# Three graph layers with the weight product behind the aggregation, without transposes, in two halves of the source tiles

## The reference, cut to what matters

```
h = relu(layernorm(x))
for i in range(3):
    hw   = h @ Ws[i]
    agg  = einsum('bij,bie->bje', adj, hw)      # A' (h W)
    h    = relu(layernorm(agg + bs[i] + h) * gammas[i] + betas[i])
x = x + h
# then: additive attention, 4-head attention, normalised graph convolution,
# each on relu(layernorm(x)) and with adj as mask or matrix
```

## Time and profile before

| what | value |
|---|---|
| median of 3 runs | 13956.94 us (13955.01 to 13957.97) |
| profiled execution, span | 13956.8 us |
| TensorE busy | 12838.3 us (92%) |
| VectorE busy | 9919.4 us (71%) |
| ScalarE busy | 9332.8 us (67%) |
| GpSimd busy | 313.1 us (2%) |
| chain that ended last: TensorE, issue, VectorE | 70%, 17%, 8% |
| adjacency products of the graph layers (L1015), busy | 1359.7 us, 3072 records |

### The profile page before, as it was taken

One profiled execution on the slowest core, in us unless ns is written; L12 is line 12 of the kernel. 1 busy time (PEld: TensorE's weight loads), 2 busy tenths in 40 slices (PEclk: granted clock), 3 DMA queues, 4 the chain that ended last, 5 costly groups with the idle time before them and its releaser, 6 DMA issues.

```text
span 13956.8 us, 273781 instructions
## 1 busy us (share of the span) xinstructions
PE 12838.3 (92%) x111489; PEld 6395.6 (46%) x111489; DVE 9919.4 (71%) x13831; ACT 9332.8 (67%) x9144; POOL 313.1 (2%) x377
## 2 busy tenths in 40 slices
PE   7998989989899898998989989899898998989989
PEld 3333843338433384333833338333383333833338
DVE  3887738877388763887638876388764887648876
ACT  2886628866288663886638866388663886638866
POOL 0000000000000000000000000000000000000000
PEclk9999989999899999999989999899999999989999
DMA  1001300013000130001300013000130001300012
GB/s 61 19 16 43 115 34 19 16 43 118 31 19 19 41 118 30 19 19 43 122 24 18 19 43 127 21 17 19 43 127 22 16 19 45 128 18 16 19 46 85
DMA packets 124596, 636.11 MB, mean 46 GB/s; under 512 B 15504, under 2 KB 49936, under 8 KB 49936
## 3 DMA queue, kind: packets, MB, share of 16 engines
q1 hardware_dynamic: 92944, 420.58, 8.6%
q0 software_dynamic: 18432, 134.23, 2.5%
q10 hardware_dynamic: 12288, 67.13, 2.3%
HBM read 546.38 MB, written 8.39 MB: 40 GB/s over the span
## 4 chain that ended last, share of the span: by engine, by line
PE 70%; issue 17%; DVE 8%; ACTq 2%; POOL 1%; ACT 1%; DMA 0%; DVEq 0%; SPq 0%; POOLq 0%
PE ps L913 44%; PE ps L955 7%; PE ps L968 4%; PE ps L926 4%; PE ps L1094 3%; PE ps L946 3%; DVE E L619 3%; ACTq L499 2%; DVE E L618 2%; PE ps L862 2%; DVE E L620 2%; PE ps L1082 1%; POOL rstd L311 1%; PE ps L977 1%; PE ps L1042 0%
## 5 line engine op out<-in xcount | busy, mean ns | idle before, releaser
L913 PE MATMUL ps<-E,a_win 128*32 128x512 f32 x65536 | 7182.0, 594 | 157.5 <-DVE E L620 88.9
L913 PEld LDWEIGHTS ps<-E,a_win 128*32 128x32 f32 x65536 | 2131.0, 110 | 5025.1 <-issue 4771.4
L404 ACT ACTIVATE E<-Q,ka 128x2048 f32<-128x2048 f32 x2048 | 4076.8, 1991 | 0.0
L403 ACT ACTIVATE E<-Q,ka 128x1024 f32<-128x1024 f32 x2048 | 2347.6, 1146 | 668.5 <-PE ps L913 666.4
L618 DVE TENSOR_SCALAR E<-Q,kd 128x2048 f32<-128x2048 f32 x2048 | 2627.6, 1283 | 186.6 <-PE ps L913 151.6
L619 DVE TENSOR_SCALAR E<-Q,kd 128x2048 f32<-128x2048 f32 x2048 | 2623.3, 1281 | 0.0
L620 DVE TENSOR_SCALAR E<-Q,kd 128x1024 f32<-128x1024 f32 x2048 | 1531.7, 748 | 0.0
L334 ACT ACTIVATE PT<-ps 128x512 f32<-128x512 f32 x1792 | 1001.9, 596 | 752.0 <-PE ps L862 478.7
L1015 PE MATMUL ps<-adj_res,HW 128*128 128x512 f32 x3072 | 1359.7, 602 | 24.0 <-ACT HW L334 16.3
L687 DVE CUSTOM_DVE_ANT_0 T<-ps,adj_ring 128x2048 f32<-128x2048 f32 x512 | 1173.3, 2292 | 251.6 <-PE ps L946 210.8
L432 ACT ACTIVATE T<-T,nmin 128x2048 f32<-128x2048 f32 x512 | 1021.9, 1996 | 304.6 <-issue 304.6
(11 more groups left out here) (111 smaller groups left out, 8100.4 us busy)
## 6 DMA issues: line engine op xcount, KB each, us to landing
adj_ring<-in_adj SPq DMA_DIRECT2D x384, 1024.0 KB, 4.8
adj_res<-in_adj POOLq DMA_DIRECT2D x128, 1024.0 KB, 6.7
qst<-qh ACTq DMA_DIRECT2D x64, 256.0 KB, 5.0
qst<-ql ACTq DMA_DIRECT2D x64, 256.0 KB, 5.0
kst<-kh ACTq DMA_DIRECT2D x64, 256.0 KB, 5.0
kst<-kl ACTq DMA_DIRECT2D x64, 256.0 KB, 5.0
X<-in_x SPq DMA_DIRECT2D x128, 64.0 KB, 1.9
out_x<-HW SPq DMA_DIRECT2D x8, 1024.0 KB, 9.7
```

Of the source, the lines that this page charges most:

```text
L403: nc.scalar.activation(E[:, s + 2, N // 2:N], Q2[:, N // 2:N], ACT.Relu, bias=ka[:, u, 32 + m:33 + m])
L404: nc.scalar.activation(E[:, s + 3, :], Q2[:, :], ACT.Relu, bias=ka[:, u, 48 + m:49 + m]).then_inc(e_act, 1)
L913: last = mm(ps[QROWS * grp:QROWS * (grp + 1), 4 * u + c, :], win, E[:, s + grp, c * CH:(c + 1) * CH], start=(m == 0), stop=(m == QUADS - 1 ...
```

## The change

The graph layers compute (A'h)W. H itself, with rows on partitions as it comes out of the relu, is the stationary operand of the adjacency products. The aggregate has features on partitions, which is what the product with W wants of its stationary operand, and that product comes out with rows on partitions. So both sets of transposes go, and so does HW as an operand; the buffer HW now holds relu(Z) + bias (`biased`), which is added to the product. The adjacency products of a layer run over all four chunks of columns with source tiles 0 to 7 first, and then over all four with tiles 8 to 15. Layer norm in the graph layers goes by chunks of four tiles. The first normalise of X goes to HT (where Z lies), so that the relu writes H from HT; the relu of the last layer moves into VectorE's residual pass. The bias table `b0` is [128, 3, 128] in place of [128, 3], and the semaphore for A is split into one for each half of its tiles.

```diff
@@ -24,16 +24,27 @@
 MASK_ADD = 1e22
 MASK_DOT = 1e9
 SCALE = float(1.0 / (HD ** 0.5))
-LNS = LAYERS + 4
-HTS = LAYERS + 2
-HEV = LAYERS + 3
+HTS = 2
+HEV = LAYERS + 2
 HALF = 8
 
 
-LN_ORDER = [(i, half) for i in range(LAYERS) for half in range(2)]
-LN_ORDER += [(LAYERS, 0), (LAYERS + 1, 0), (LAYERS, 1), (LAYERS + 1, 1)]
-LN_ORDER += [(i, half) for i in range(LAYERS + 2, LNS) for half in range(2)]
-DVE_STEPS = 2 * LNS + 4 * LAYERS + 7
+def half_of(half):
+    return range(half * HALF, (half + 1) * HALF)
+
+
+def chunk_of(c):
+    return range(c * TPC, (c + 1) * TPC)
+
+
+LN_X, LN_1, LN_2, LN_3 = 0, LAYERS + 1, LAYERS + 2, LAYERS + 3
+LN_STEPS = [(LN_X, half_of(half)) for half in range(2)]
+LN_STEPS += [(l, chunk_of(c)) for l in range(1, LAYERS) for c in range(NC)]
+LN_STEPS += [(i, chunk_of(c)) for c in range(NC) for i in (LAYERS, LN_1)]
+LN_STEPS += [(i, half_of(half)) for i in (LN_2, LN_3) for half in range(2)]
+LN_COUNT = len(LN_STEPS)
+LN_EARLY = LN_COUNT - 4
+DVE_STEPS = 68
 STEPS = NT * HEADS
 
 
...
@@ -360,16 +368,9 @@
                 evac_ht(b, i, 3)
                 after(3)
 
-            def evac_hw(b, l, g):
-                if l == 0 and g == 0:
-                    act.wait_ge(out_done, b * 16 + 16)
-                act.wait_ge(hw_ps, b * (LAYERS * NC) + l * NC + g + 1)
-                evac(HW[:, g * CH:(g + 1) * CH], ps[:, 4 + g, :]).then_inc(hw_sb, 1)
-
             def evac_agg(b, l, c):
                 act.wait_ge(agg_ps, b * (LAYERS * NC) + l * NC + c + 1)
-                nc.scalar.activation(AGG[:, c * CH:(c + 1) * CH], ps[:, c, :], ACT.Identity,
-                                     bias=b0[:, l:l + 1]).then_inc(agg_sb, 1)
+                evac(AGG[:, c * CH:(c + 1) * CH], ps[:, c, :]).then_inc(agg_sb, 1)
 
             def evac_q1(b, c):
                 act.wait_ge(qk1_ps, b * 6 + c + 1)
@@ -461,19 +462,21 @@
             act.sem_inc(hb_sb, NT)
             with act.Fori(0, NB) as b:
                 Hf = H[:, :, :].rearrange("p t d -> p (t d)")
-                h_section(b, 0, 0, Hf, lambda g: evac_hw(b, 0, g))
+                for g in range(NC):
+                    relu(b, 0, HT, g)
                 for l in range(LAYERS):
-                    for c in range(NC - 1):
+
+                    evac_agg(b, l, 0)
+                    evac_agg(b, l, 1)
+                    for c in range(2, NC):
+                        if l < LAYERS - 1:
+                            relu(b, l + 1, HT, c - 2)
                         evac_agg(b, l, c)
                     if l < LAYERS - 1:
-                        h_section(b, l + 1, l + 1, HT, lambda g: evac_hw(b, l + 1, g), lambda: evac_agg(b, l, NC - 1))
-                    else:
-                        for g in range(NC):
-                            if g == 2:
-                                evac_agg(b, l, NC - 1)
-                            relu(b, LAYERS, HT, g)
-
-                h_section(b, LAYERS, LAYERS + 1, Hf, lambda c: evac_q1(b, c))
+                        relu(b, l + 1, HT, 2)
+                        relu(b, l + 1, HT, 3)
+
+                h_section(b, 0, LAYERS, Hf, lambda c: evac_q1(b, c))
                 for c in range(2):
                     act.wait_ge(qk1_ps, b * 6 + 4 + c + 1)
                     evac(K2[:, c * CH:(c + 1) * CH], ps[:, c, :]).then_inc(qk1_sb, 1)
...
@@ -553,49 +556,67 @@
             nc.vector.tensor_copy(w1t2[:, DG:P], ps[:, 0, 0:DG])
             nc.vector.tensor_copy(w2t[:, :], ps[:, 0, DG:P]).then_inc(const_rdy, 1)
 
-            def tiles_of(half):
-                return range(half * HALF, (half + 1) * HALF)
-
-            def norm_stats(b, half, src):
-
-                for t in tiles_of(half):
+            def ln_at(i, over):
+                return LN_STEPS.index((i, over)) + 1
+
+            def norm_stats(b, over, src):
+
+                for t in over:
                     last = nc.vector.bn_stats(stats[:, t, :], src[:, t, :])
                 link(b, last)
                 alone(dve)
-                for t in tiles_of(half):
+                for t in over:
                     last = nc.vector.bn_aggr(mv[:, t, :], stats[:, t, :])
                 last.then_inc(ln_stats, 1)
 
-            def normalise(b, i, half, src, dst, done):
-
-                dve.wait_ge(ln_rstd, b * (2 * LNS) + LN_ORDER.index((i, half)) + 1)
-                for t in tiles_of(half):
+            def normalise(b, i, over, src, dst, done):
+
+                dve.wait_ge(ln_rstd, b * LN_COUNT + ln_at(i, over))
+                for t in over:
                     last = nc.vector.tensor_scalar(dst[:, t, :], src[:, t, :], mv[:, t, 0:1], rstd[:, t:t + 1],
                                                    ALU.subtract, ALU.mult)
                     if t % TPC == TPC - 1:
                         last.then_inc(done, 1)
 
-            def normalise_affine(b, i, half, Z, l):
-
-                for t in tiles_of(half):
+            def centre(b, i, over, Z, l):
+
+                dve.wait_ge(ln_stats, b * LN_COUNT + ln_at(i, over))
+                for t in over:
                     last = nc.vector.scalar_tensor_tensor(out=Z[:, t, :], in0=Z[:, t, :], scalar=mv[:, t, 0:1],
                                                           in1=gam[:, l, :], op0=ALU.subtract, op1=ALU.mult)
                 link(b, last)
-                dve.wait_ge(ln_rstd, b * (2 * LNS) + LN_ORDER.index((i, half)) + 1)
-                for t in tiles_of(half):
+
+            def rescale(b, i, over, Z, l):
+
+                dve.wait_ge(ln_rstd, b * LN_COUNT + ln_at(i, over))
+                for t in over:
                     last = nc.vector.scalar_tensor_tensor(out=Z[:, t, :], in0=Z[:, t, :], scalar=rstd[:, t:t + 1],
                                                           in1=bet[:, l, :], op0=ALU.mult, op1=ALU.add)
-                    if t % TPC == TPC - 1:
-                        last.then_inc(zn_rdy, 1)
-
-            def residual(b, half):
-
-                for g in (2 * half, 2 * half + 1):
-                    dve.wait_ge(h_rdy, (b * HEV + LAYERS) * NC + g + 1)
-                    xg = X[:, g * TPC:(g + 1) * TPC, :]
-                    last = nc.vector.tensor_tensor(xg, xg, H[:, g * TPC:(g + 1) * TPC, :], ALU.add)
-                link(b, last)
-                norm_stats(b, half, X)
+                return last
+
+            def chunk(buf, c):
+                return buf[:, c * TPC:(c + 1) * TPC, :]
+
+            def biased(b, l, c, Z, HB):
+
+                dve.wait_ge(zn_rdy, (b * HEV + l) * NC + c + 1)
+                row = b0[:, l, :].rearrange("p (o d) -> p o d", o=1).broadcast_to([P, TPC, D])
+                return nc.vector.scalar_tensor_tensor(out=chunk(HB, c), in0=chunk(Z, c), scalar=0.0, in1=row,
+                                                      op0=ALU.max, op1=ALU.add)
+
+            def conv(b, l, c, Z, HB):
+
+                dve.wait_ge(z_ps, b * (LAYERS * NC) + l * NC + c + 1)
+                link(b, nc.vector.tensor_tensor(
+                    chunk(Z, c), ps[:, 4 + c, :].rearrange("p (t d) -> p t d", d=D), chunk(HB, c), ALU.add))
+                norm_stats(b, chunk_of(c), Z)
+                centre(b, l + 1, chunk_of(c), Z, l)
+
+            def residual(b, c, Z):
+
+                link(b, nc.vector.scalar_tensor_tensor(out=chunk(X, c), in0=chunk(Z, c), scalar=0.0, in1=chunk(X, c),
+                                                       op0=ALU.max, op1=ALU.add))
+                norm_stats(b, chunk_of(c), X)
 
             def tiles(buf):
...
@@ -751,29 +772,28 @@
             own.k = 0
             with dve.Fori(0, NB) as b:
                 dve.wait_ge(x_in, (b + 1) * (16 * NT))
+                Z, HB = tiles(HT), tiles(HW)
                 for half in range(2):
-                    norm_stats(b, half, X)
+                    norm_stats(b, half_of(half), X)
                 for half in range(2):
-                    normalise(b, 0, half, X, H, zn_rdy)
-                Z = tiles(HT)
-                for l in range(LAYERS):
-
-                    for half in range(2):
-                        for g in (2 * half, 2 * half + 1):
-                            dve.wait_ge(z_ps, b * (LAYERS * NC) + l * NC + g + 1)
-                            last = nc.vector.tensor_tensor(
-                                Z[:, g * TPC:(g + 1) * TPC, :],
-                                ps[:, 4 + g, :].rearrange("p (t d) -> p t d", d=D),
-                                H[:, g * TPC:(g + 1) * TPC, :], ALU.add)
-                        link(b, last)
-                        norm_stats(b, half, Z)
-                        dve.wait_ge(ln_stats, b * (2 * LNS) + LN_ORDER.index((l + 1, half)) + 1)
-                        normalise_affine(b, l + 1, half, Z, l)
-                        if l == LAYERS - 1 and half == 0:
-                            residual(b, 0)
-                normalise(b, LAYERS + 1, 0, X, H, zn_rdy)
-                residual(b, 1)
-                normalise(b, LAYERS + 1, 1, X, H, zn_rdy)
```

(70 more changed lines are left out.)

39 lines of the change are left out of this document (17 added, 22 removed).

## The result

The changed kernel takes 13522.87 us (median of 4 runs, 13513.81 to 13528.44), the kernel before 13955.98 us on the same chip. The ratio is 0.9685, with the 95% interval from 0.9673 to 0.9697. The profiled executions span 13526.8 and 13956.8 us. The forecast was 13,570 us with a range from 13,535 to 13,635; the kernel gained 433 us where 388 were forecast.

A forecast was written before the change was run, and what follows sets the result against it. TensorE, busy 92% of the span, was taken as the bound. A batch's graph layers at 202.8 us gave 332 us over batches two to eight plus 56 in the first: 13956.9 - 388, called 13,570 us; range 13,535 to 13,635.

The forecast's parts named there:

- Everything behind 2041.30 is the same code in both kernels: From the second batch's first attention product on, nothing was taken to change; no gain was counted there.
- another time of the attention stage: Listed sign of a wrong prediction: the attention stage takes another time than before; no size given.
- the section ahead of layer 0: Start of each batch: transposes and products with W before the adjacency products go, 13.95 us.
- the end of the layers: From the last adjacency product to the first attention product: 23.9 us, where it was 32.59.
- the first four terms: After the last adjacency products: 0.94 + 0.93 + 0.1 us to the last W products' end, then VectorE 0.5 late.
- The rest of the way: From the last normalise to the first attention product: 11.7 us, where it was 13.37.
- the cold start: TensorE's low clock after the idle stretch before a batch: 2.0 us charged once per batch.
- W products against transposes: Per 512 columns, four products with W replace four transposes of AGG: 0.93 us in place of 0.44.
- Rival C: The page's fourfold ratio for transposes holds: 10 us more per batch, 80 in all, 13,650 us; chance 0.03.
- VectorE (B): VectorE's four-tile chain is longer and falls behind in the last layer: 48 us, 13,618 us; chance 0.10.
- ScalarE's order (E): Relus ahead of copies make TensorE wait mid-layer if VectorE's chain is late: slower than before, 13,990 us; chance 0.03.
- the prediction's rival D: First batch gains nothing from adjacency halves, which land together: 20 us back, 13,590 us; chance 0.07.

The follow-up runs named there:

- the runs with increments: Semaphore increments on TensorE, once, ahead of the batch loop: 52 in the kernel before, 13915.72 us; 204 in the changed kernel, 13577.97 us.
- the run with the whole adjacency: The changed kernel with layer 0 waiting for all 16 adjacency tiles before its first product: 13560.71 us, in a second run 13563.49.

## Why the prediction was wrong

**The step that failed** is in the first paragraph: "Everything behind 2041.30 is the same code in both kernels", from which the sum took its time as the same. The instructions are the same, their place in TensorE's code is not. It was worth 47.5 us in the profiled executions, and the runs with increments showed it in both directions. The prediction named another time of the attention stage among what would prove it wrong, but without a mechanism or a price. The Trainium skill's page on the runtime, cited above, has the rule about branches; the prediction did not draw on it, nor on the instruction queue or the pitch of the tiles (62.7 us where 61.51 was possible). By the profiled spans the 430.0 us of gain are 378.2 in the graph layers, 10 less than forecast, 47.5 in the attention stage, where none was forecast, and 4.6 in the other stretches. The first two errors have opposite signs, so the total hides part of each. With its loop where the kernel before has it, the changed kernel took 13577.97 us, within the forecast's range.

**The graph layers** were right in mechanism, and near in size: 378.2 us of gain, 388 forecast. By terms: the section ahead of layer 0 goes, as said. A layer takes 59.46 us (59.58). Two terms were too small. The first is the end of the layers. From the last adjacency product to the end of the last normalise the sum has 0.94 + 0.93 + 0.1 + 0.5 + 7.5 + 1.2 + 1.07 = 12.24 us; it took 13.0 in every batch, 0.3 for the first four terms and 0.5 for the chain, in which the power took 1.01 us. The rest of the way took 11.6 to 12.3 us (11.7). Together, the second batch takes 24.6 us from the end of its last adjacency product (1902.31 + 5.32 - 0.17 = 1907.46) to the attention, the eight 25.1 in the mean (23.9 forecast), 9.5 us in all. The second is the clock's: 2.0 us per batch for the cold start, where layer 0 took 62.0 to 62.6 us in six of the eight batches, 2.6 to 3.1 over the later layers, and 61.0 and 61.1 in two, 2.6 in the mean, 4.6 us in all. The layers themselves gave 0.3 us per batch back. The granted clock in windows of the changed kernel's second batch, before and behind its first product, answers to the earlier trace rows:
```profile
1723.00:1729.28 6.28, 0.01 (x1) 0.01 (x1) 5.98 (x40) 0.63 (x1) 3.42 (x4) 0.50 0.79 325
1729.28:1733.50 4.22, 4.22 (x6) 1.89 (x7) 4.14 (x13) 1.89 (x3) 0.35 (x1) 0.63 0.00 0
1733.50:1740.00 6.50, 6.50 (x17) 2.91 (x16) 0.71 (x2) 0.00 (x0) 0.00 (x0) 1.00 0.00 0
```
0.50 is the 1.2 GHz level; the second row holds both levels. The prediction took the price of the second batch of the kernel before for all.

**W products against transposes:** 0.89 us for eight records, as the row of before said. By the factor of four of the Trainium skill's page that the prediction names it would have been 1.76; the measurement decides, for products with 128 columns and a new stationary tile each. Rival C falls.

**VectorE (B) and ScalarE's order (E)** did not come about. VectorE waited 2.29 us between chunks in layer 1, and the only idle time inside a layer is the 0.69 us for the last copy.

**The first batch (the prediction's rival D)** started at 44.61: the halves of the transfer land apart, and the run with the whole adjacency gave the 20 us back.

**The net worth of the change.** With the loop written out in both kernels, place does not enter: 13448.70 against 13857.96 us, 409 us. The profiled executions differ by 403.5 us: 377 in the graph layers, 28 in the stretches with the convolution stage, which vary, 3 behind the last attention stretch and -6 in the attention products.

## What to carry to other kernels

When code is removed ahead of a loop that TensorE is bound by, look at the first hundred instructions behind the loop's turn, and at the packets of the instruction queue there: holes in the weight loads there move with the code, and a stage that "doesn't change" can give or take as much as a small edit. A change is best measured against its rival at equal place, or with such a loop written out. The runs hold three places of the loop, so how much a place can cost at most is not known. The order (A'h)W with H as the stationary operand needs no transposes on either side, and the layer norm hid behind the next chunks here, its chain per chunk being shorter than their pitch of 7.76 us.

## What the runs showed of the hardware

- Code is moved in packets of 16,384 bytes, one for some 255 records of TensorE's straight code. Behind the turn of TensorE's loop the load stream had a hole of 0.60 to 1.39 us in place of 0.29 where the code lay badly; it ended 1.18 to 1.58 us behind the landing of a packet of code. A turn that lay well still cost 1.6 us against straight code (989.7 against 979.9 us per batch, 6 turns).
- 52 instructions that do nothing, ahead of the batch loop, gave 39 us of 13,955.
- GpSimd's power takes 1.01 us for 4 columns, 1.66 for 8 and 3.71 for 16.
- The seven stretches with the convolution stage varied between 3455 and 3488 us in the profiled executions, with the attention products of a batch steady to within 3 us in each kernel. Why was not tried and stays open.
